# Graph aggregation with LayerNorm: row tiles in groups of twelve instead of eight, a ring of three 48 KB slots instead of eight of 16 KB, programs written out without loops

## The chip, the cores and the metric

The kernel runs on one core of a Trainium2 chip. The metric is device time in microseconds (us) for one execution; lower is better. Times of whole runs are medians over several executions; the profile comes from one execution of its own.

## The reference

`x` is 8192 x 64, `adj` is 8192 x 8192, both float32, `w` has 8192 entries and `W_agg` is 64 x 64.

```python
agg = adj @ (x @ W_agg)
y = x + w[:, None] * relu(agg) + (1 - w)[:, None] * x
out = (y - mean(y)) / sqrt(var(y) + 1e-5)      # over the 64 columns of a row
```

`adj` is 268 MB and is read once; everything else together is some 4 MB.

## The kernel before

The 8192 rows of the result are 64 row tiles of 128 rows. The contraction over 8192 columns of `adj` is cut into 64 steps `j` of 128. Before the launch the host lays `adj` out so that each transfer reads one contiguous row of bytes per partition.

**Head.** SP loads `x` in four transfers (L107) and `W_agg` twice (L109, L110), then fills the ring (L115). For eight blocks TensorE (PE) transposes two row tiles of `x` at a time (`transpose_x`, L156), ScalarE (ACT) copies the transposed block out of PSUM (L225), PE multiplies it with `W_agg` (L172), and VectorE (DVE) copies the product into `xw` (L258). Both PSUM stages have two buffers, so block b waits for the copy of block b-2. ACT loads `w` (L220) after the first transposes; DVE waits for it only after the eighth block (L261).

**Main stage.** Seven groups of eight row tiles. A group is 16 loads of 2 MB (`SUB` = 4 steps `j`, 16 KB per partition) into a ring of eight slots. `contract` (L177) multiplies: for each `j` the 128 x 64 block of `xw` is the weight, and two halves of the row tiles, 512 columns each, stream past it into the two halves of the partitions of `acc`. One float32 product shows as two MATMUL records and two LDWEIGHTS. The last one of a load frees its slot (`slot_free`), on which SP waits before it issues the load eight places on (L119). Then a group of six row tiles follows (16 loads of 1.5 MB, L126), and one of two (six loads of 2, 2, 2, 1, 0.5 and 0.5 MB, L133).

**End of a group.** ACT copies `acc` out (L231), PE turns it back with transposes (`turn_back`, L194), and DVE and ACT finish: residual, weighting, mean, variance, square root, reciprocal, scaling (L271 to L290). ACT stores the rows (L236). PE goes on with the next group as soon as its transposes are issued.

The order on each queue is that of the program. SP issues nothing but loads, ACT the load of `w` and the stores. The main groups are hardware loops (`Fori`) on SP, PE, ACT and DVE.

Of the kernel before, what the change touches and what calls it, by code (L numbers as in the profile page):

```python
# [17 lines left out]
def gnn_residual_layernorm(nc, x, adj_main, adj_mid, adj_last, w, w_agg, out):  # L18

# [20 lines left out]
    PAIRS = T // 2  # L40
    PB = 4
    BLOCKS = PAIRS // PB
    LOADS = (G + 1) * C + len(LAST_LOADS)
    assert C * SUB == T == sum(LAST_LOADS) and LAST_T0 + LAST_SLOTS == T and C % RING == 0

    DVE_PRE = 1
    DVE_GROUP = 9
    VSUM_STEP = 8

    def arrivals(load):  # L50

        return 16 * (load // RING + 1)

    ctx = ExitStack()
    with ctx:
# [36 lines left out]
        xT_done, xT_copied = sem("xT_done"), sem("xT_copied")
        xw_done, xw_copied = sem("xw_done"), sem("xw_copied")
        agg_copied = sem("agg_copied")
# [7 lines left out]
        @block.sync  # L102
        def _(sp):

            for i in range(X_PARTS):
                part = slice(i * T // X_PARTS, (i + 1) * T // X_PARTS)
                sp.dma_start(xres[:, part], x.rearrange("(p t) d -> p t d", p=P)[:, part]).then_inc(x_in[i], 16)  # L107
                if i == 0:
                    sp.dma_start(wagg2[0:D, :], w_agg).then_inc(wagg_in, 16)  # L109
                    sp.dma_start(wagg2[D:P, :], w_agg).then_inc(wagg_in, 16)  # L110
            for c in range(C):
                if c >= RING:

                    sp.wait_ge(slot_free, c - RING + 1)
                sp.dma_start(ring[:, c % RING], adj_main[0, c].rearrange("q s n -> q (s n)")).then_inc(loaded[c % RING], 16)  # L115
            with sp.Fori(1, G) as g:
                for c in range(C):

                    sp.wait_ge(slot_free, g * C + (c - RING + 1))  # L119
                    sp.dma_start(ring[:, c % RING],  # L120
                                 adj_main[bass.ds(g, 1), c].rearrange("o q s n -> (o q) (s n)")).then_inc(loaded[c % RING], 16)
            for c in range(C):
                load = MID * C + c

                sp.wait_ge(slot_free, load - RING + 1)
# [21 lines left out]
        def _(pe):  # L147
            def transpose_x(b):

                if b % (BLOCKS // X_PARTS) == 0:  # L150
                    pe.wait_ge(x_in[b * X_PARTS // BLOCKS], 16)
                if b >= 2:
                    pe.wait_ge(xT_copied, b - 1)
                for i in range(PB):
                    t = 2 * (b * PB + i)
                    last = nc.tensor.transpose(xT_ps[b % 2][:, i * P:(i + 1) * P],  # L156
                                               xres[:, t:t + 2].rearrange("p t d -> p (t d)"), ident[:])
                last.then_inc(xT_done, 1)

            pe.wait_ge(ident_ready, 1)
            transpose_x(0)
# [25 lines left out]
            def turn_back(g, n_slots):  # L188

# [3 lines left out]
                for k in range(n_slots // HALVES):  # L193
# [4 lines left out]
            with pe.Fori(0, G) as g:  # L198
                for c in range(C):
                    pe.wait_ge(loaded[c % RING], g * (16 * C // RING) + arrivals(c))  # L200
                    contract(c % RING, c * SUB, SUB, MAIN_SLOTS)
                turn_back(g, MAIN_SLOTS)
            for c in range(C):
                load = MID * C + c
                pe.wait_ge(loaded[load % RING], arrivals(load))
                contract(load % RING, c * SUB, SUB, MID_SLOTS)
            turn_back(MID, MID_SLOTS)
            j = 0
            for i, n in enumerate(LAST_LOADS):
                load = LAST * C + i  # L210
                pe.wait_ge(loaded[load % RING], arrivals(load))
                contract(load % RING, j, n, LAST_SLOTS)
                j += n
            turn_back(LAST, LAST_SLOTS)

        @block.scalar
        def _(act):

            act.wait_ge(xT_done, 1)
            act.dma_start(w_sb[:], w.rearrange("(p t) -> p t", p=P)).then_inc(w_in, 16)  # L220
            for b in range(BLOCKS):
# [3 lines left out]
                nc.scalar.copy(xT[:, b % 2], xT_ps[b % 2][:]).then_inc(xT_copied, 1)  # L225
            act.wait_ge(eps_ready, 1)

            def group(g, t0, n_slots, loads):
                width = n_slots // HALVES * P
                act.wait_ge(slot_free, loads)  # L230
                nc.scalar.copy(aggT[:, 0:width], acc[:, 0:width]).then_inc(agg_copied, 1)  # L231
                act.wait_ge(dve_step, g * DVE_GROUP + (DVE_PRE + VSUM_STEP))
                nc.scalar.activation(std[:, 0:n_slots], varsum[:, 0:n_slots], ACT.Sqrt,  # L233
                                     bias=eps[:, 0:1], scale=1.0 / D).then_inc(std_ready, 1)
                act.wait_ge(out_ready, g + 1)
                act.dma_start(out.rearrange("(p t) d -> p t d", p=P)[:, bass.ds(t0, n_slots)],  # L236
                              xres[:, bass.ds(t0, n_slots)]).then_inc(stored, 16)

            with act.Fori(0, G) as g:
                group(g, g * MAIN_SLOTS, MAIN_SLOTS, g * C + C)  # L240
            group(MID, MID_T0, MID_SLOTS, LAST * C)
            group(LAST, LAST_T0, LAST_SLOTS, LOADS)
# [3 lines left out]
        def _(dve):  # L246
            def step(instruction, count):

# [5 lines left out]

            for b in range(BLOCKS):
                dve.wait_ge(xw_done, b + 1)
                for h in range(2):
                    last = nc.vector.tensor_copy(xw[:, 2 * PB * b + h:2 * PB * (b + 1):2], xw_ps[b % 2][h][:])  # L258
# [4 lines left out]
            for i in range(X_PARTS):  # L263
                dve.wait_ge(x_in[i], 16)
            dve.wait_ge(xT_done, BLOCKS)

            def group(g, t0, n):
                base = g * DVE_GROUP + DVE_PRE
                v, s, residual = y[:, 0:n], sq[:, 0:n], xres[:, bass.ds(t0, n)]

                step(nc.vector.tensor_tensor(s, residual, over_row(one_minus_w[:, bass.ds(t0, n)]), ALU.mult), base + 1)  # L271
                step(nc.vector.tensor_tensor(residual, residual, s, ALU.add), base + 2)  # L272
                dve.wait_ge(rows_done, g + 1)

                step(nc.vector.scalar_tensor_tensor(out=v, in0=rows_ps[:, 0:n * D].rearrange("p (n d) -> p n d", d=D),  # L275
# [53 lines left out]
```

## Time and profile before

| | us |
|---|---|
| median of 3 runs | 653.82 (653.77 to 653.98) |
| span of the profiled execution, first to last instruction | 651.5 |
| busy: PE / weight loads / DVE / ACT | 496.9 / 174.3 / 58.3 / 31.4 |
| DMA: bytes moved, mean rate over the span | 272.84 MB, 419 GB/s |

The profile gives no time of its own for its execution other than the span; the median of the runs stands 2.3 us above it. In the rows below a time is in us from the start of the span unless marked ns. SPq and ACTq are the queues on which SP and ACT issue transfers; q1 holds SP's transfers, q10 ACT's, q8 the engines' instruction fetches. Text in square brackets behind an instruction is how long its engine had been idle and what ended that.

### The profile page before, as it was taken

The numbers are of one execution on the slowest core, as the hardware profiler recorded it, in microseconds if no ns is written. First come the engines' busy times: TensorE is split into PE (matmuls) and PEld (weight loads), VectorE is DVE, ScalarE is ACT, GpSimd is POOL, SyncE is SP. The second block draws the span as 40 slices with busy tenths as digits, with TensorE's granted clock in tenths as the row PEclk, the third lists the DMA queues.
The fourth block names the chain that finished last, engine by engine and source line by source line (L and its number), as shares of the span: only waits on it lengthen the run. The fifth ranks groups of instructions, "written<-read, shape, count | busy, mean of one in ns | idle before, by whom it ended". The sixth has DMA issues, their size and how long they took to land.

```text
span 651.5 us, 5854 instructions
## 1 busy us (share of the span) xinstructions
PE 496.9 (76%) x2496; PEld 174.3 (27%) x2496; DVE 58.3 (9%) x107; ACT 31.4 (5%) x41; POOL 0.7 (0%) x7
## 2 busy tenths in 40 slices
PE   6999887677777778767777777877777777777775
PEld 5733222222222122222222212212222221222245
DVE  1300012000210003000030000300003000030021
ACT  2200010000100001000020000200002000100000
POOL 0000000000000000000000000000000000000000
PEclk9999999999999999999999999999999999999999
DMA  8999999999999999999999999999999999999994
GB/s 316 433 427 428 430 424 431 432 423 433 430 426 432 425 430 433 424 431 431 425 433 423 431 433 424 428 434 426 432 424 432 432 424 432 426 425 428 422 429 164
DMA packets 21481, 272.84 MB, mean 419 GB/s; under 512 B 2656, under 2 KB 2912, under 8 KB 4576
## 3 DMA queue, kind: packets, MB, share of 16 engines
q1 hardware_dynamic: 20032, 270.57, 97.8%
q10 hardware_dynamic: 1440, 2.13, 0.9%
q8 instruction: 7, 0.11, 0.1%
q14 instruction: 2, 0.02, 0.0%
HBM read 270.60 MB, written 2.10 MB: 419 GB/s over the span
## 4 chain that ended last, share of the span: by engine, by line
DMA 80%; PE 18%; issue 0%; DVE 0%; ACT 0%; SPq 0%; ACTq 0%; DVEq 0%
DMA ring<-adj_main_dram 65%; PE acc L184 15%; DMA ring<-adj_mid_dram 9%; DMA ring<-adj_last_dram 5%; PE xw_ps L172 2%; PE xT_ps L156 1%; DMA xres<-x_dram 1%; ACT L225 0%; SPq L120 0%; ACT xT L225 0%; DVE xw L258 0%; ACTq L220 0%; PE rows_ps L194 0%; ACT std L233 0%; DVE y L279 0%
## 5 line engine op out<-in xcount | busy, mean ns | idle before, releaser
L184 PE MATMUL acc<-ring,xw 128*64 128x512 f32 (+2 forms) x2304 | 468.4, 552 | 137.3 <-DMA ring<-adj_main_dram 119.6
L184 PEld LDWEIGHTS acc<-ring,xw 128*64 128x64 f32 x2304 | 151.0, 137 | 449.2 <-issue 217.9
L275 DVE SCALAR_TENSOR_TENSOR y<-rows_ps,w_sb 128x512 f32<-128x512 f32 (+2 forms) x9 | 5.7, 632 | 560.3 <-PE rows_ps L194 560.3
L231 ACT COPY aggT<-acc 128x512 f32<-128x512 f32 (+2 forms) x9 | 4.8, 538 | 550.8 <-PE acc L184 550.8
L172 PE MATMUL xw_ps<-wagg,xT 64*128 64x64 f32 x128 | 15.5, 424 | 0.7 <-ACT xT L225 0.7
L172 PEld LDWEIGHTS xw_ps<-wagg,xT 64*128 64x128 f32 x128 | 14.2, 326 | 3.1 <-issue 2.0
L156 PE MATMUL xT_ps<-ident,xres 128*128 128x128 f32 x32 | 8.9, 433 | 5.3 <-DMA xres<-x_dram 4.8
L194 PE MATMUL rows_ps<-ident,aggT 128*128 128x128 f32 x32 | 5.4, 288 | 6.3 <-ACT aggT L231 6.3
L231 ACT ACT_TABLE_LOAD x7 | 9.0, 1283 | 11.5 <-DVE xres L290 11.4
L233 ACT ACT_TABLE_LOAD x7 | 9.0, 1283 | 0.1
L258 DVE COPY xw<-xw_ps 128x256 f32<-128x256 f32 x16 | 6.0, 419 | 24.4 <-PE xw_ps L172 24.4
L156 PEld LDWEIGHTS xT_ps<-ident,xres 128*128 128x128 f32 x32 | 5.7, 216 | 6.4 <-issue 4.8
L194 PEld LDWEIGHTS rows_ps<-ident,aggT 128*128 128x128 f32 x32 | 3.4, 140 | 13.3 <-issue 11.5
L279 DVE TENSOR_TENSOR y<-y,xres 128x512 f32<-128x512 f32 (+2 forms) x9 | 5.7, 633 | 0.3
L290 DVE TENSOR_TENSOR xres<-y,rstd 128x512 f32 (+2 forms) x9 | 5.7, 633 | 0.3
L272 DVE TENSOR_TENSOR xres<-xres,sq 128x512 f32 (+2 forms) x9 | 5.7, 632 | 0.3
L285 DVE TENSOR_TENSOR sq<-y 128x512 f32<-128x512 f32 (+2 forms) x9 | 5.7, 632 | 0.3
L282 DVE SCALAR_TENSOR_TENSOR y<-rowsum,y 128x512 f32<-128x512 f32 (+2 forms) x9 | 5.7, 632 | 0.3
L286 DVE TENSOR_REDUCE varsum<-sq 128x8 f32<-128x512 f32 (+2 forms) x9 | 5.6, 627 | 0.3
L281 DVE TENSOR_REDUCE rowsum<-y 128x8 f32<-128x512 f32 (+2 forms) x9 | 5.6, 627 | 0.3
L271 DVE TENSOR_TENSOR sq<-xres,one_minus_w 128x512 f32 (+2 forms) x9 | 5.6, 626 | 0.4 <-DVE one_minus_w L262 0.4
L225 ACT COPY xT<-xT_ps 128x512 f32<-128x512 f32 x8 | 4.6, 586 | 14.5 <-PE xT_ps L156 14.4
(11 smaller groups left out, 6.9 us busy)
## 6 DMA issues: line engine op xcount, KB each, us to landing
ring<-adj_main_dram SPq DMA_DIRECT2D x112, 2048.0 KB, 35.3
ring<-adj_mid_dram SPq DMA_DIRECT2D x16, 1536.0 KB, 27.5
ring<-adj_last_dram SPq DMA_DIRECT2D x3, 2048.0 KB, 29.0
xres<-x_dram SPq DMA_DIRECT2D x4, 512.0 KB, 6.3
out_dram<-xres ACTq DMA_DIRECT2D x7, 256.0 KB, 9.4
ring<-adj_last_dram SPq DMA_DIRECT2D x1, 1024.0 KB, 29.5
ring<-adj_last_dram SPq DMA_DIRECT2D x2, 512.0 KB, 25.8
out_dram<-xres ACTq DMA_DIRECT2D x1, 192.0 KB, 7.8
```

Source lines behind the costliest of these rows:

```text
L156: last = nc.tensor.transpose(xT_ps[b % 2][:, i * P:(i + 1) * P], xres[:, t:t + 2].rearrange("p t d -> p (t d)"), ident[:])
L172: last = nc.tensor.matmul(xw_ps[b % 2][h][:, i], xT[h * D:(h + 1) * D, b % 2, i * P:(i + 1) * P], wagg2[h * D:(h + 1) * D, :], start=True, ...
L184: last = nc.tensor.matmul(acc[h * D:(h + 1) * D, 0:width], xw[:, j], ring[:, slot, at:at + width], start=j == 0, stop=j == T - 1)
L194: last = nc.tensor.transpose(rows_ps[:, k * P:(k + 1) * P], aggT[:, k * P:(k + 1) * P], ident[:])
L231: nc.scalar.copy(aggT[:, 0:width], acc[:, 0:width]).then_inc(agg_copied, 1)
L233: nc.scalar.activation(std[:, 0:n_slots], varsum[:, 0:n_slots], ACT.Sqrt, bias=eps[:, 0:1], scale=1.0 / D).then_inc(std_ready, 1)
L258: last = nc.vector.tensor_copy(xw[:, 2 * PB * b + h:2 * PB * (b + 1):2], xw_ps[b % 2][h][:])
L272: step(nc.vector.tensor_tensor(residual, residual, s, ALU.add), base + 2)
L275: step(nc.vector.scalar_tensor_tensor(out=v, in0=rows_ps[:, 0:n * D].rearrange("p (n d) -> p n d", d=D), scalar=0.0, in1=over_row(w_sb[:, ...
L279: step(nc.vector.tensor_tensor(v, v, residual, ALU.add), base + 4)
L282: step(nc.vector.scalar_tensor_tensor(out=v, in0=over_row(rowsum[:, 0:n]), scalar=-1.0 / D, in1=v, op0=ALU.mult, op1=ALU.add), base + 6)
L285: step(nc.vector.tensor_tensor(s, v, v, ALU.mult), base + 7)
```

## The change

- Main groups of twelve row tiles (five groups of eight loads). A load is 6 MB: eight steps `j`, 48 KB per partition. The ring has three slots.
- A group of three row tiles (nine loads, 1.5 MB each but for the last two), and a last one of a single row tile, whose ten shrinking transfers all go into one ring slot and have a semaphore each. For these two groups, even and odd `j` go to the two halves of the partitions, and a product with two stacked identities adds the halves while it turns them back.
- A main load is 8 x 4 products of 384 columns, over two PSUM banks.
- `x` comes in one transfer. The two loads of `W_agg` move from SP to ACT, and the load of `w` moves to ACT's first instructions, behind them. DVE waits for `w` before the first copy of `xw`.
- `(2 - w) * x` is computed once for all rows, relu is applied by ACT in its copy for the main groups, and the square-root table of ACT is loaded once, at the start.
- The last row tile uses `bn_stats` and `bn_aggr`.
- No hardware loops.

The diff, cut to its core:

```diff
-HALVES = 2
-MAIN_SLOTS = 8
-MID_SLOTS = 6
-LAST_SLOTS = 2
-SUB = 4
-LAST_LOADS = (16, 16, 16, 8, 4, 4)
-RING = 8
-X_PARTS = 4
+HALVES = 1
+MAIN_SLOTS = 12
+MID_SLOTS = 3
+LAST_SLOTS = 1
+SUB = 8
+RING = 3
+MID_LOADS = (8, 8, 8, 8, 8, 8, 8, 5, 3)
+LAST_LOADS = (16, 13, 10, 7, 5, 4, 3, 2, 2, 2)
...
         def _(sp):
-            for i in range(X_PARTS):
-                part = slice(i * T // X_PARTS, (i + 1) * T // X_PARTS)
-                sp.dma_start(xres[:, part], x.rearrange("(p t) d -> p t d", p=P)[:, part]).then_inc(x_in[i], 16)
-                if i == 0:
-                    sp.dma_start(wagg2[0:D, :], w_agg).then_inc(wagg_in, 16)
-                    sp.dma_start(wagg2[D:P, :], w_agg).then_inc(wagg_in, 16)
...
+            sp.dma_start(xres[:], x.rearrange("(p t) d -> p t d", p=P)).then_inc(x_in, 16)
+            for load in range(G * C):
+                if load >= RING:
+                    sp.wait_ge(slot_free, load - RING + 1)
+                sp.dma_start(ring[:, load % RING],
+                             adj_main[load // C, load % C].rearrange("q s n -> q (s n)")).then_inc(loaded[load % RING], 16)
+            j = 0
+            for i, n in enumerate(MID_LOADS):
+                load = MID_LOAD0 + i
                 sp.wait_ge(slot_free, load - RING + 1)
+                sp.dma_start(ring[:, load % RING, 0:n * MID_SLOTS * P],
+                             adj_mid[j // SUB, :, j % SUB:j % SUB + n].rearrange("q s n -> q (s n)")
+                             ).then_inc(loaded[load % RING], 16)
+                j += n
+            sp.wait_ge(slot_free, LAST_LOAD0 - RING + 1)
             j = 0
+            for k, n in enumerate(LAST_LOADS):
+                sp.dma_start(ring[:, LAST_LOAD0 % RING, j * P:(j + n) * P],
+                             adj_last[:, j:j + n].rearrange("q s n -> q (s n)")).then_inc(last_loaded[k], 16)
                 j += n
...
-            def contract(slot, j0, n_j, n_slots):
-                width = n_slots // HALVES * P
-                for s in range(n_j):
+            def contract(slot, j0):
+                for s in range(SUB):
                     j = j0 + s
-                    for h in range(HALVES):
-                        at = (s * HALVES + h) * width
-                        last = nc.tensor.matmul(acc[h * D:(h + 1) * D, 0:width], xw[:, j], ring[:, slot, at:at + width],
-                                                start=j == 0, stop=j == T - 1)
+                    for b in range(BANKS):
+                        for h in range(2):
+                            at = s * COLS + (h * BANKS + b) * CHUNK
+                            last = nc.tensor.matmul(acc[h * D:(h + 1) * D, b, 0:CHUNK], xw[:, j], ring[:, slot, at:at + CHUNK],
+                                                    start=j == 0, stop=j == T - 1)
                 last.then_inc(slot_free, 1)
...
         def _(act):
-            act.wait_ge(xT_done, 1)
+            for h in range(2):
+                act.dma_start(wagg2[h * D:(h + 1) * D, :], w_agg).then_inc(wagg_in, 16)
             act.dma_start(w_sb[:], w.rearrange("(p t) -> p t", p=P)).then_inc(w_in, 16)
+            nc.scalar.preload_act_table_set("sqrt_and_others")
...
         def _(dve):
+            dve.wait_ge(ident_ready, 1)
+            nc.vector.tensor_tensor(ident2[:], ident[:, 0:D], ident[:, D:P], ALU.add).then_inc(ident2_ready, 1)
+            dve.wait_ge(w_in, 16)
+            step(nc.vector.tensor_scalar(two_minus_w[:], w_sb[:], -1.0, 2.0, ALU.mult, ALU.add), 1)
             for b in range(BLOCKS):
                 dve.wait_ge(xw_done, b + 1)
...
-            dve.wait_ge(w_in, 16)
-            step(nc.vector.tensor_scalar(one_minus_w[:], w_sb[:], -1.0, 1.0, ALU.mult, ALU.add), DVE_PRE)
...
+            step(nc.vector.tensor_tensor(xres[:], xres[:], over_row(two_minus_w[:]), ALU.mult), DVE_PRE)
...
+            v, t = y[:, 0], LAST_T0
+            dve.wait_ge(rows_done, LAST + 1)
+            step(nc.vector.tensor_scalar(v, rows_ps[:, 0:D], 0.0, w_sb[:, t:t + 1], ALU.max, ALU.mult), LAST_STEP0 + 1)
+            step(nc.vector.tensor_tensor(v, v, xres[:, t], ALU.add), LAST_STEP0 + 2)
+            step(nc.vector.bn_stats(stats[:], v), LAST_STEP0 + 3)
+            step(nc.vector.bn_aggr(mv[:], stats[:]), LAST_STEP0 + LAST_VAR_STEP)
+            dve.wait_ge(std_ready, LAST + 1)
+            step(nc.vector.reciprocal(rstd[:, 0:1], std[:, 0:1]), LAST_STEP0 + 5)
+            nc.vector.tensor_scalar(xres[:, t], v, mv[:, 0:1], rstd[:, 0:1], ALU.subtract, ALU.mult).then_inc(out_ready, 1)
```

## Rows read from the trace of the kernel before

**Rows 1.** The page: DMA share by slice; instruction queue (packets, MB, share); chain by engine.

```profile
DMA  8999999999999999999999999999999999999994
...
q8 instruction: 7, 0.11, 0.1%
...
DMA 80%; PE 18%; issue 0%; DVE 0%; ACT 0%; SPq 0%; ACTq 0%; DVEq 0%
```

**Rows 2.** The chain of waits in order of time: start, duration, what.

```profile
0.74 3.90 DMA xres<-x_dram
...
105.07 3.68 PE acc L184 x16
...
144.83 3.68 PE acc L184 x16
...
183.98 3.68 PE acc L184 x16
```

**Rows 3.** Timeline of the group of six row tiles: start, duration, instruction.

```profile
614.58 0.82 PE L184 MATMUL acc<-ring,xw 128*64 128x384 f32 x4
...
616.29 2.80 PE L184 MATMUL acc<-ring,xw 128*64 128x384 f32 x16 [0.89 <-DMA ring<-adj_mid_dram]
...
623.67 2.80 PE L184 MATMUL acc<-ring,xw 128*64 128x384 f32 x16 [0.90 <-DMA ring<-adj_mid_dram]
...
626.52 0.48 ACT L231 COPY aggT<-acc 128x384 f32<-128x384 f32 x1 [52.87 <-PE acc L184]
...
627.05 0.55 PE L194 MATMUL rows_ps<-ident,aggT 128*128 128x128 f32 x3 [0.58 <-ACT aggT L231]
```

**Rows 4.** DMA issues: size in KB, median us from issue to landing.

```profile
out_dram<-xres ACTq DMA_DIRECT2D x7, 256.0 KB, 9.4
...
out_dram<-xres ACTq DMA_DIRECT2D x1, 64.0 KB, 1.6
...
w_sb<-w_dram ACTq DMA_DIRECT2D x1, 32.0 KB, 10.8
```

**Rows 5.** Timeline of the head, PE and the ring's first issues.

```profile
3.99 6.15 SPq L115 DMA_DIRECT2D ring<-adj_main_dram  x8
...
8.24 1.97 PE L172 MATMUL xw_ps<-wagg,xT 64*128 64x64 f32 x16 [0.70 <-ACT xT L225]
...
14.14 1.97 PE L172 MATMUL xw_ps<-wagg,xT 64*128 64x64 f32 x16
...
30.66 19.69 PE L184 MATMUL acc<-ring,xw 128*64 128x512 f32 x80 [1.04 <-DVE xw L258]
```

**Rows 6.** Stretches of the head: window, length, busy (count) by engine, PEclk, DMA share, GB/s.

```profile
4.00:5.00 1.00, 0.22 (x1) 0.25 (x2) 0.00 (x0) 0.00 (x0) 0.00 (x0) 1.00 0.61 99
5.00:6.00 1.00, 0.87 (x4) 0.46 (x3) 0.00 (x0) 0.00 (x0) 0.00 (x0) 1.00 0.70 214
...
30.60:35.40 4.80, 4.74 (x12) 1.52 (x14) 1.39 (x2) 0.00 (x0) 0.00 (x0) 1.00 0.99 423
35.40:60.00 24.60, 24.60 (x116) 8.19 (x114) 0.00 (x0) 0.00 (x0) 0.00 (x0) 1.00 1.01 429
```

**Rows 7.** Timeline of the last group.

```profile
633.46 3.71 PE L184 MATMUL acc<-ring,xw 128*64 128x128 f32 x64 [1.18 <-DMA ring<-adj_last_dram]
...
638.63 7.21 PE L184 MATMUL acc<-ring,xw 128*64 128x128 f32 x128 [1.45 <-DMA ring<-adj_last_dram]
645.88 0.27 ACT L231 COPY aggT<-acc 128x128 f32<-128x128 f32 x1 [14.33 <-PE acc L184]
...
646.96 0.29 DVE L279 TENSOR_TENSOR y<-y,xres 128x128 f32<-128x128 f32 x1
...
649.50 0.36 ACTq L236 DMA_DIRECT2D out_dram<-xres  x1
```

**Rows 8.** Stretches of the end, columns as in rows 6.

```profile
640.00:641.00 1.00, 1.00 (x24) 1.00 (x22) 0.00 (x0) 0.00 (x0) 0.00 (x0) 1.00 0.85 336
...
643.00:644.00 1.00, 1.00 (x22) 1.00 (x20) 0.00 (x0) 0.00 (x0) 0.00 (x0) 1.00 0.02 8
...
650.00:652.00 2.00, 0.00 (x0) 0.00 (x0) 0.00 (x0) 0.00 (x0) 0.00 (x0) 0.50 0.11 33
```

More of the change, by code:

```diff
@@ L39, in gnn_residual_layernorm @@
     COLS = MAIN_SLOTS * P
[L40 to L48, printed above, removed]
+    HALF = MAIN_SLOTS // 2
+    BANKS = 2
+    CHUNK = HALF * P // BANKS
+    MID_BANKS = -(-MID_SLOTS * P // 512)
+    MID_CHUNK = MID_SLOTS * P // MID_BANKS
+    BLOCKS = T // 2 // PB
+    MID_LOAD0 = G * C
+    LAST_LOAD0 = MID_LOAD0 + len(MID_LOADS)
+    assert C * SUB == T == sum(MID_LOADS) == sum(LAST_LOADS) and LAST_T0 + LAST_SLOTS == T
+    DVE_PRE = 2
+    DVE_GROUP, VAR_STEP = 7, 6
+    LAST_STEP0 = DVE_PRE + LAST * DVE_GROUP
+    LAST_VAR_STEP = 4
     def arrivals(load):
@@ L186, in contract, with turn_back @@
                 last.then_inc(slot_free, 1)
-            def turn_back(g, n_slots):
+            def turn_back(g):
                 pe.wait_ge(agg_copied, g + 1)
                 pe.wait_ge(dve_step, g * DVE_GROUP + DVE_PRE)
-                for k in range(n_slots // HALVES):
+                for k in range(HALF):
                     last = nc.tensor.transpose(rows_ps[:, k * P:(k + 1) * P], aggT[:, k * P:(k + 1) * P], ident[:])
                 last.then_inc(rows_done, 1)
-            with pe.Fori(0, G) as g:
+            for g in range(G):
@@ L214, in _ @@
-            turn_back(LAST, LAST_SLOTS)
+                    load = g * C + c
+                    pe.wait_ge(loaded[load % RING], arrivals(load))
+                    contract(load % RING, c * SUB)
+                turn_back(g)
+            j = 0
+            for i, n in enumerate(MID_LOADS):
+                load = MID_LOAD0 + i
+                pe.wait_ge(loaded[load % RING], arrivals(load))
+                for s in range(n):
+                    h = (j + s) % 2
+                    for b in range(MID_BANKS):
+                        at = s * MID_SLOTS * P + b * MID_CHUNK
+                        last = nc.tensor.matmul(mid_acc[h * D:(h + 1) * D, b, 0:MID_CHUNK], xw[:, j + s],
+                                                ring[:, load % RING, at:at + MID_CHUNK], start=j + s < 2, stop=j + s >= T - 2)
+                last.then_inc(slot_free, 1)
+                j += n
@@ new lines, in _ @@
+            j = 0
+            for k, n in enumerate(LAST_LOADS):
+                pe.wait_ge(last_loaded[k], 16)
+                for s in range(n):
+                    h = (j + s) % 2
+                    last = nc.tensor.matmul(last_acc[h * D:(h + 1) * D, 0:P], xw[:, j + s],
+                                            ring[:, LAST_LOAD0 % RING, (j + s) * P:(j + s + 1) * P],
+                                            start=j + s < 2, stop=j + s >= T - 2)
+                j += n
+                if k == 0:
+                    pe.wait_ge(ident2_ready, 1)
+                    pe.wait_ge(agg_copied, MID + 1)
+                    pe.wait_ge(dve_step, MID * DVE_GROUP + DVE_PRE)
+                    for i in range(MID_SLOTS):
+                        turned = nc.tensor.matmul(rows_ps[:, i * D:(i + 1) * D], aggT[:, i * P:(i + 1) * P], ident2[:],
+                                                  start=True, stop=True)
+                    turned.then_inc(rows_done, 1)
@@ L224, in _ @@
                     act.wait_ge(xw_done, b - 1)
-                nc.scalar.copy(xT[:, b % 2], xT_ps[b % 2][:]).then_inc(xT_copied, 1)
+                nc.scalar.copy(xT[:, b % 2], xT_ps[:, b % 2]).then_inc(xT_copied, 1)
             act.wait_ge(eps_ready, 1)
[L228 to L234, printed above, removed]
-                act.wait_ge(out_ready, g + 1)
-                act.dma_start(out.rearrange("(p t) d -> p t d", p=P)[:, bass.ds(t0, n_slots)],
-                              xres[:, bass.ds(t0, n_slots)]).then_inc(stored, 16)
@@ L239, in _, with finish @@
[L239 to L242, printed above, removed]
+            out_rows = out.rearrange("(p t) d -> p t d", p=P)
+            def finish(g, t0, n_slots, var, scale, var_step):
+                act.wait_ge(dve_step, var_step)
+                nc.scalar.activation(std[:, 0:n_slots], var, ACT.Sqrt, bias=eps[:, 0:1], scale=scale).then_inc(std_ready, 1)
+                act.wait_ge(out_ready, g + 1)
+                act.dma_start(out_rows[:, t0:t0 + n_slots], xres[:, t0:t0 + n_slots]).then_inc(stored, 16)
@@ new lines, in _ @@
+            for g in range(G):
+                act.wait_ge(slot_free, g * C + C)
+                nc.scalar.activation(aggT[:].rearrange("p (b n) -> p b n", b=BANKS), acc[:, :, 0:CHUNK],
+                                     ACT.Relu).then_inc(agg_copied, 1)
+                finish(g, g * MAIN_SLOTS, MAIN_SLOTS, varsum[:], 1.0 / D, g * DVE_GROUP + (DVE_PRE + VAR_STEP))
+            act.wait_ge(slot_free, LAST_LOAD0)
+            nc.scalar.copy(aggT[:, 0:MID_SLOTS * P].rearrange("p (b n) -> p b n", b=MID_BANKS),
+                           mid_acc[:, 0:MID_BANKS, 0:MID_CHUNK]).then_inc(agg_copied, 1)
@@ L243, in _ @@
+            finish(MID, MID_T0, MID_SLOTS, varsum[:, 0:MID_SLOTS], 1.0 / D, MID * DVE_GROUP + DVE_PRE + VAR_STEP)
+            act.wait_ge(last_done, 1)
+            nc.scalar.copy(aggT[:, 0:P], last_acc[:, 0:P]).then_inc(agg_copied, 1)
+            finish(LAST, LAST_T0, 1, mv[:, 1:2], 1.0, LAST_STEP0 + LAST_VAR_STEP)
             act.wait_ge(stored, 16 * (LAST + 1))
@@ L257, in _ @@
                 for h in range(2):
[L258 removed]
+                    last = nc.vector.tensor_copy(xw[:, 2 * PB * b + h:2 * PB * (b + 1):2], xw_ps[b % 2][h])
                 last.then_inc(xw_copied, 1)
[L261 to L264 removed]
@@ L265, in _, with normalise @@
             dve.wait_ge(xT_done, BLOCKS)
-            def group(g, t0, n):
+            step(nc.vector.tensor_tensor(xres[:], xres[:], over_row(two_minus_w[:]), ALU.mult), DVE_PRE)
+            def normalise(g, t0, n, base):
+                v, s, residual = y[:, 0:n], sq[:, 0:n], xres[:, t0:t0 + n]
+                step(nc.vector.tensor_tensor(v, v, residual, ALU.add), base + 2)
+                step(nc.vector.tensor_reduce(rowsum[:, 0:n], v, AX.X, ALU.add), base + 3)
+                step(nc.vector.scalar_tensor_tensor(out=v, in0=over_row(rowsum[:, 0:n]), scalar=-1.0 / D, in1=v,
+                                                    op0=ALU.mult, op1=ALU.add), base + 4)
+                step(nc.vector.tensor_tensor(s, v, v, ALU.mult), base + 5)
+                step(nc.vector.tensor_reduce(varsum[:, 0:n], s, AX.X, ALU.add), base + VAR_STEP)
+                dve.wait_ge(std_ready, g + 1)
+                step(nc.vector.reciprocal(rstd[:, 0:n], std[:, 0:n]), base + DVE_GROUP)
+                nc.vector.tensor_tensor(residual, v, over_row(rstd[:, 0:n]), ALU.mult).then_inc(out_ready, 1)
@@ L268, in group @@
+            for g in range(G):
                 base = g * DVE_GROUP + DVE_PRE
-                v, s, residual = y[:, 0:n], sq[:, 0:n], xres[:, bass.ds(t0, n)]
-                step(nc.vector.tensor_tensor(s, residual, over_row(one_minus_w[:, bass.ds(t0, n)]), ALU.mult), base + 1)
-                step(nc.vector.tensor_tensor(residual, residual, s, ALU.add), base + 2)
                 dve.wait_ge(rows_done, g + 1)
-                step(nc.vector.scalar_tensor_tensor(out=v, in0=rows_ps[:, 0:n * D].rearrange("p (n d) -> p n d", d=D),
-                                                    scalar=0.0, in1=over_row(w_sb[:, bass.ds(t0, n)]),
-                                                    op0=ALU.max, op1=ALU.mult), base + 3)
@@ L287, in group @@
-                dve.wait_ge(std_ready, g + 1)
-                step(nc.vector.reciprocal(rstd[:, 0:n], std[:, 0:n]), base + 9)
-                nc.vector.tensor_tensor(residual, v, over_row(rstd[:, 0:n]), ALU.mult).then_inc(out_ready, 1)
-            with dve.Fori(0, G) as g:
-                group(g, g * MAIN_SLOTS, MAIN_SLOTS)
-            group(MID, MID_T0, MID_SLOTS)
-            group(LAST, LAST_T0, LAST_SLOTS)
+                for h in range(2):
+                    slots = slice(g * MAIN_SLOTS + h * HALF, g * MAIN_SLOTS + (h + 1) * HALF)
+                    last = nc.vector.tensor_tensor(
+                        y[:, h * HALF:(h + 1) * HALF],
+                        rows_ps[:, 0:MAIN_SLOTS * D].rearrange("p (k h d) -> p h k d", h=2, d=D)[:, h],
+                        over_row(w_sb[:, slots]), ALU.mult)
@@ new lines, in _ @@
+                step(last, base + 1)
+                normalise(g, g * MAIN_SLOTS, MAIN_SLOTS, base)
+            base = MID * DVE_GROUP + DVE_PRE
+            dve.wait_ge(rows_done, MID + 1)
+            step(nc.vector.scalar_tensor_tensor(out=y[:, 0:MID_SLOTS],
+                                                in0=rows_ps[:, 0:MID_SLOTS * D].rearrange("p (n d) -> p n d", d=D),
+                                                scalar=0.0, in1=over_row(w_sb[:, MID_T0:LAST_T0]),
+                                                op0=ALU.max, op1=ALU.mult), base + 1)
```

72 lines of the change are left out of this document (25 added, 47 removed).

## The prediction

> **What bounds the kernel now.** I read the page's slices first: the DMA engines are busy nine tenths or more in every slice but the first and the last, and the chain that ended last is 80% DMA [rows 1]. The time is therefore the time that the bytes take, plus what precedes the first byte, plus what follows the last, plus any hole in between. The chain in order of time gives the pace: eight loads of 2 MB take 183.98 - 144.83 = 39.15 us, 4.894 us each; with one 256 KB store among them it is 39.76 [rows 2], so a store costs what its bytes cost. PE waits for a transfer at every load: a load of 1.5 MB keeps it 2.80 us out of 3.69 [rows 3]. Its own speed matters only where it decides when a ring slot comes free and the queue has run short. So I look for what changes in the rate, at both ends, and for holes.
>
> **The rate.** 128 rows over 16 DMA engines are 8 rows per engine and load. A 16 KB row takes 4.894 / 8 = 0.6118 us [rows 2], a 12 KB row 3.69 / 8 = 0.4612, the pitch of two loads being 623.67 - 616.29 [rows 3]. The difference, 0.1506 us for 4 KB, is the price of bytes; 0.6118 - 4 x 0.1506 = 0.009 us is left per row. (At this accuracy the intercept is 0.007 to 0.011.) Rows per engine before: 8 x (112 + 16 + 6 + 4) = 1104; after: 8 x (40 + 9 + 10 + 1) = 480. Gain 624 x 0.009 = **-5.6 us**, at the same bytes. A 48 KB row is then 12 x 0.1506 + 0.009 = 1.816 us and a 6 MB load 14.53. No row above 16 KB is in this trace, so the bounds are 0 (a long row is moved in pieces) and -6.9.
>
> **x in one transfer.** The four issues of x, with the two of W_agg among them, leave the engines 39% and 30% idle in the fifth and sixth microsecond [rows 6]. With x and the first load issued back to back that goes: **-0.7 us** (0 to -0.8).
>
> **Instruction fetch.** Before, 7 fetches bring 0.11 MB [rows 1]. Without loops PE's program grows: its instructions went from 2 x 2496 executed, of which six of seven passes of a body of 512 were not fetched again (some 1900 in all), to about 6000. In proportion that is 0.25 MB more: **+0.6 us** if it falls on all engines alike, up to 5 if few of them carry it; at the end the engines finish up to 3 us apart [rows 8], so they are not loaded alike. PE uses some 130 instructions per 14.5 us, so no fetch is waited for. I find no row of a loop's back edge on the chain; removing loops gains nothing.
>
> **The tail.** The engines run out at 643 [rows 8], and PE's 128 last products run without a wait from 638.63 to 645.84 [rows 7]: the end is PE's, not the last transfer's. From 645.88 to the store's issue at 649.50 are 3.6 us, and the landing 1.6 more [rows 4] and a little to the end of the span. After: the last load is two steps, four records; by (7.21 - 3.71) / 64 = 0.055 us each and some 0.2 us for the pipeline that is 0.5 us, with 0.5 for the landing's way to PE. Then the same chain with two VectorE steps fewer (bn_stats and bn_aggr for reduce, subtract, square, reduce), 0.33 each by the pitch of [rows 7]; bn_aggr is in no row, and I take both for one step each (bounds: half, or twice). 643 + 1.0 + 3.0 + 2.0 = 649.0 instead of 651.5: **-2.5 us** (-1.8 to -3.2).
>
> **Hole at the end of the main groups.** This is the new wait that I trust most. Of one load's 64 records at 384 columns each takes (2.80 - 0.82) / 12 = 0.165 us [rows 3], so PE holds a 6 MB slot for 0.82 + 60 x 0.165 = 10.7 us. When the last main load lands, the other two slots hold loads of the next group, 2 x 3.69 = 7.4 us of transfer; the third waits, on SP's queue, for those 10.7 us. From a free slot to the first byte, and from the last byte to the waiter, together cost about 1.6 us (the last store, alone on the queue, [rows 4]; the first part of x took 3.90 for 1.2 us of bytes [rows 2], so up to 2.7). Idle: 10.7 + 1.6 - 7.4 = 4.9 us. Next PE turns the group back before it frees another slot: copy and transposes took 1.1 us for 384 columns of `acc` [rows 3], about 1.75 for 768; with 2.8 for the load, 4.55 against 3.69 of transfer: 0.9. The last ten transfers wait for one slot: landing 0.5, PE 2.8, issue 1.1, against 3.7 us still queued (loads of 5 and 3 steps): 0.7. Together **+6.5 us** (5 to 9).
>
> **Hole behind the head.** DVE now waits for w ahead of its first copy of xw; behind that wait stand all eight pairs of copies, and PE's third block waits for the first of them, because the PSUM stage has two buffers. w is the third transfer on ACT's queue. After, W_agg twice and w are 4 + 4 + 8 = 16 turns, and each turn beside a 48 KB row is 1.82 us. x fills about 2 to 7 us. Earliest: the first eight turns run beside x, w's eight beside the ring: 7 + 8 x 1.82 + 0.5 = 22. Latest: the first turn comes 2.9 us late, 12.7 turns are left when x is through: 30.6. I take the middle, 26. From block 2 on the head is PE's as before, 30.66 - 14.14 = 16.5 us [rows 5]; with 1.0 for DVE's first work PE starts the main loop at 43.5 (39.5 to 48), against 30.66. Its first 4.8 us run at half rate, as now: 12 records in 4.8 us and then 116 in 24.6 [rows 6]. The first slot is free 10.7 + 2.2 us later and its load's first byte 1.1 after that: 57.5. The queue holds x and three loads, 1.9 + 4.9 + 43.6 and some 1.6 for the engine that is last: dry at 52. Idle: **+5.5 us** (1.5 to 10). If w came before 21 us, PE would start in time (by 38 us, x itself only costs it some 2 us: landed at about 8.3, and ACT's table load is gone), and the hole would be 0.
>
> What I cost at nothing: relu in ACT's copy, the hoisted (2 - w)x (4.4 us on DVE), the longer group ends; under them lies 14.5 - 10.7 = 3.8 us of PE slack per load. Without that slack they would cost their 1 to 2 us five times.
>
> **Sum.** -5.6 - 0.7 + 0.6 - 2.5 + 6.5 + 5.5 = +3.8 on the profiled 651.5, which lies 2.3 under the median of the runs: 655.3 there, **657.6 us** as a median. With the bounds of the head's hole alone, 653.6 to 662.1.
>
> **A rule that speaks otherwise.** [Rows 4] say one row per turn. The Trainium skill, "DMA: Bandwidth & Descriptors", section on queues, rings and completion order, has a DMA engine drain a whole packet, typically 9 to 17 descriptors, from one ring before it switches. By that, w's eight rows would come in one turn, the head's hole would be 0 and the sum 652.1. The 9.4 against 1.6 us speak against it.
>
> **Rivals.** (1) *The head is covered* (ends on the other side): ACT's small rows get in ahead of the ring, w lands before 21 us. For it: ACT's queue starts at the same moment as SP's, and nothing in this trace shows a 48 KB row. Against it: [rows 4]. Without the hole: -1.7, 652.1, just faster. 25%. (2) *Long rows are moved in pieces* of at most 16 KB: no gain in rate, but turns stay at 0.61 us and w lands at 13; -0.7 + 0.6 - 2.5 + 6.5 = +3.9, 657.7, from another cause. 10%. (3) *PE's clock and the fetches*: the granted clock fell to half, 0.50, after PE's end at 646.5 [rows 8]; after the change PE idles 3.8 us per load instead of 1.2. If the clock falls ahead of the last main load, its slot comes 2.2 us later, and fetches that pile up on few engines add 2 to 4: 662 to 664. 10%. The forecast has the remaining 55%.
>
> **Numbers.** 0.2% is 1.3 us, about what a measurement of this kernel can tell from no change: faster below 652.5, slower above 655.1. Rival 1 is faster in two thirds of its cases and the same in the rest; the forecast's low end gives 5% to faster, 10% to no change. Faster 0.22, same 0.18, slower 0.60. The range reaches down to rival 1 with a shorter hole at the group end and up to the late w: 650.8 to 662.5; the likeliest case's own is 653.6 to 662.1.
>
> **What would show it.** Right: q1 rows of 48 KB at 27 GB/s per engine; w landing 20 to 30 us after its issue; DVE's first copy of xw waiting for it; first main product near 43; DMA share dropping for some 5 us at 52, and again some 7 us after the last main load lands; PE idle 3.8 us per main load; DMA's end about 6 us before the end of the span. Wrong: main products from 33 on (rival 1); a main load at 14.7 us (rival 2); main records at twice their length ahead of the last group (rival 3). A hole at the group end under 3 us, or none, would make the sum wrong by as much.

## The result and the profile after

| | us |
|---|---|
| before, median of 4 runs | 653.9 (653.77 to 654.04) |
| after, median of 4 runs | 673.1 (671.91 to 675.26) |
| ratio after to before | 1.030, 95% interval 1.028 to 1.032 |
| span of the profiled execution after | 670.1 |

The change makes the kernel 19 us slower; 657.6 was forecast. The direction and the places were right, the sizes were not. The page of the kernel after: the DMA share by slice and the rate, which answer to [rows 1], with PE's granted clock, and the instruction fetches.

```profile
PEclk9999989889788989889998979898979898989998
DMA  9992999999999999999999999999999999997795
GB/s 377 448 429 86 432 423 432 449 429 426 438 423 428 441 437 426 428 439 421 440 444 428 421 428 438 429 434 441 429 428 429 432 429 446 426 425 291 250 365 232
...
q8 instruction: 23, 0.38, 0.2%
```

Two places stand out: the fourth slice (86 GB/s) and the four last. Between them the rate is 421 to 449 GB/s, about as before. The granted clock is below nine tenths in 18 of the 40 slices, which it never was before. The chain of waits in order of time (start, duration, what), which answers to [rows 2], says what stood at these places:

```profile
1.95 30.35 DMA w_sb<-w_dram
...
49.79 44.04 PE bank L179 x256
...
568.39 10.56 PE bank L179 x64
...
612.00 10.56 PE bank L179 x64
622.59 0.82 ACT aggT L258
623.41 0.04 issue
623.45 0.87 PE bank L188 x6
...
635.74 4.22 PE bank L206 x16
```

The head is now a wait of 30 us for `w`, 32 KB, and the main products begin at 49.8 where they began at 30.7 [rows 5]. At the end the last main load holds its slot until 622.6. The stretches at both places (window, length, busy and count of PE, PEld, DVE, ACT and POOL, granted clock, DMA share, GB/s):

```profile
48.00:52.00 4.00, 3.14 (x18) 1.74 (x18) 3.05 (x4) 0.00 (x0) 0.00 (x0) 1.00 0.57 246
52.00:56.00 4.00, 4.00 (x18) 1.44 (x17) 2.07 (x1) 0.00 (x0) 0.00 (x0) 1.00 0.00 0
56.00:60.00 4.00, 4.00 (x28) 1.73 (x26) 0.00 (x0) 0.00 (x0) 0.00 (x0) 1.00 0.02 4
60.00:64.00 4.00, 4.00 (x28) 1.71 (x26) 0.00 (x0) 0.00 (x0) 0.00 (x0) 1.00 0.38 111
64.00:68.00 4.00, 4.00 (x28) 1.79 (x26) 0.00 (x0) 0.00 (x0) 0.00 (x0) 1.00 0.72 283
...
612.00:616.00 4.00, 4.00 (x26) 1.85 (x28) 0.00 (x0) 0.00 (x0) 0.00 (x0) 1.00 0.84 353
616.00:620.00 4.00, 4.00 (x28) 1.79 (x26) 0.00 (x0) 0.00 (x0) 0.00 (x0) 1.00 0.12 52
620.00:624.00 4.00, 3.09 (x21) 1.41 (x18) 0.00 (x0) 0.81 (x1) 0.00 (x0) 1.00 0.12 28
624.00:628.00 4.00, 4.00 (x28) 1.86 (x27) 3.53 (x5) 0.00 (x0) 0.00 (x0) 1.00 0.92 351
628.00:632.00 4.00, 4.00 (x28) 1.57 (x23) 3.46 (x5) 0.30 (x1) 0.00 (x0) 1.00 0.86 261
```

The DMA engines are idle while PE is fully busy. That is what a ring looks like that has run dry because PE holds the slots. Summed over the first five windows (4 x (0.43 + 1.00 + 0.98 + 0.62 + 0.28)) a mean engine loses 13.2 us at the head, over the last five 8.6.

### The profile page after: what moved, and what is told of

Read it like the earlier page. It is cut to its first block, busy times and chain, and to the rows that moved or that the text cites. A ratio compares the mean times of both kernels' runs of the same rounds, so it can differ in the third digit from the quotient of the medians.

```text
span 670.1 us, 6264 instructions
## 1 busy us (share of the span) xinstructions
PE 523.6 (78%) x3014; PEld 233.9 (35%) x3014; DVE 49.7 (7%) x78; ACT 12.9 (2%) x23; POOL 0.7 (0%) x7
## 3 DMA queue, kind: packets, MB, share of 16 engines
q10 hardware_dynamic: 1312, 2.16, 0.8%
## 4 chain that ended last, share of the span: by engine, by line
DMA 66%; PE 33%; DVE 0%; issue 0%; ACT 0%; ACTq 0%; DVEq 0%
DMA ring<-adj_main_dram 58%; PE bank L179 27%; DMA w_sb<-w_dram 5%; DMA ring<-adj_mid_dram 2%; PE bank L168 2%; PE bank L206 1%; PE bank L215 1%; DMA ring<-adj_last_dram 1%; PE bank L152 1%; DVE xw L286 0%; ACTq L237 0%; PE bank L188 0%; ACT aggT L258 0%; PE bank L225 0%; PE bank L232 0%
## 5 line engine op out<-in xcount | busy, mean ns | idle before, releaser
L179 PE MATMUL bank<-ring,xw 128*64 128x384 f32 x2560 | 462.4, 524 | 104.0 <-DMA ring<-adj_main_dram 103.2
L179 PEld LDWEIGHTS bank<-ring,xw 128*64 128x64 f32 x2560 | 192.0, 147 | 372.2 <-issue 245.9
L206 PE MATMUL bank<-ring,xw 128*64 128x384 f32 x128 | 23.1, 514 | 6.0 <-DMA ring<-adj_mid_dram 6.0
L168 PE MATMUL bank<-wagg,xT 64*128 64x64 f32 x128 | 15.5, 423 | 8.8 <-DVE xw L286 8.8
L152 PE MATMUL bank<-ident,xres 128*128 128x128 f32 x32 | 8.9, 433 | 16.6 <-DMA xres<-x_dram 8.6
L168 PEld LDWEIGHTS bank<-wagg,xT 64*128 64x128 f32 x128 | 14.2, 325 | 11.1 <-issue 11.1
L206 PEld LDWEIGHTS bank<-ring,xw 128*64 128x64 f32 x128 | 9.3, 144 | 19.3 <-issue 10.2
L152 PEld LDWEIGHTS bank<-ident,xres 128*128 128x128 f32 x32 | 5.7, 217 | 17.7 <-issue 8.6
L215 PE MATMUL bank<-ring,xw 128*64 128x128 f32 x128 | 9.1, 311 | 2.2 <-DMA ring<-adj_last_dram 2.2
L215 PEld LDWEIGHTS bank<-ring,xw 128*64 128x64 f32 x128 | 8.5, 158 | 2.9 <-DMA ring<-adj_last_dram 2.9
L286 DVE COPY xw<-bank 128x256 f32<-128x256 f32 x16 | 6.0, 419 | 11.3 <-PE bank L168 11.2
L302 DVE TENSOR_TENSOR xres<-y,rstd 128x768 f32<-128x768 f32 (+1 forms) x6 | 5.2, 858 | 0.2
L294 DVE TENSOR_TENSOR y<-y,xres 128x768 f32<-128x768 f32 (+1 forms) x6 | 5.2, 858 | 0.2
```

What stands on the lines that cost most here:

```text
L152: last = nc.tensor.transpose(xT_ps[:, b % 2, i * P:(i + 1) * P], xres[:, t:t + 2].rearrange("p t d -> p (t d)"), ident[:])
L168: last = nc.tensor.matmul(xw_ps[b % 2][h][:, i], xT[h * D:(h + 1) * D, b % 2, i * P:(i + 1) * P], wagg2[h * D:(h + 1) * D, :], start=True, ...
L179: last = nc.tensor.matmul(acc[h * D:(h + 1) * D, b, 0:CHUNK], xw[:, j], ring[:, slot, at:at + CHUNK], start=j == 0, stop=j == T - 1)
L206: last = nc.tensor.matmul(mid_acc[h * D:(h + 1) * D, b, 0:MID_CHUNK], xw[:, j + s], ring[:, load % RING, at:at + MID_CHUNK], start=j + s < ...
L215: last = nc.tensor.matmul(last_acc[h * D:(h + 1) * D, 0:P], xw[:, j + s], ring[:, LAST_LOAD0 % RING, (j + s) * P:(j + s + 1) * P], start=j ...
L294: step(nc.vector.tensor_tensor(v, v, residual, ALU.add), base + 2)
```

## The experiments

Three theories stood against each other. **A**: these two holes are the loss. **B**: the loss is PE's clock, which was granted at 0.93 on average instead of 1.00. **C**: the longer programs, written out without loops, bring fetches that delay the transfers. The first two runs each undo one part of the change, the third alters the ring, and the fourth takes one part of the change into the kernel before.

**e1: only the wait moves.** VectorE waits for `w` behind the copies of `xw` again.

```diff
         def _(dve):
...
-            dve.wait_ge(w_in, 16)
-            step(nc.vector.tensor_scalar(two_minus_w[:], w_sb[:], -1.0, 2.0, ALU.mult, ALU.add), 1)
             for b in range(BLOCKS):
...
+            dve.wait_ge(w_in, 16)
+            step(nc.vector.tensor_scalar(two_minus_w[:], w_sb[:], -1.0, 2.0, ALU.mult, ALU.add), 1)
             dve.wait_ge(xT_done, BLOCKS)
```

> Only VectorE's wait for w (with the small product that needs it) goes back behind the eight copies of xw. Theory A (holes in the transfers: the ring runs dry at 53 us because the head waits for w): W_agg still lands at 17 us on ACT's queue, so PE's first product stays at 18.7, but the main products start 22.4 later, at 41, instead of 49.8; the first slot is free at 54.7 and the hole shrinks from 11.5 to about 3 us: 673.1 - 8.6 = 664.5 us. Theory B (the loss is PE at half clock, the granted mean being 0.93): the clock in the main stage is as before, and the time stays within 1 us of 673.

Measured: 664.1 us (661.95 to 664.41), 9.0 less than after. The timeline has the first main products at 41.1, as A had it:

```profile
41.10 39.38 PE L179 MATMUL bank<-ring,xw 128*64 128x384 f32 x226 [0.86 <-DVE xw L284]
```

The mean clock is still 0.93, so the clock did not bring these 9 us back: B falls for this part.

**e2: only the queue moves.** `W_agg` and `w` are issued by SP, behind `x` and ahead of the ring; the wait stays where the change put it.

```diff
             sp.dma_start(xres[:], x.rearrange("(p t) d -> p t d", p=P)).then_inc(x_in, 16)
+            for h in range(2):
+                sp.dma_start(wagg2[h * D:(h + 1) * D, :], w_agg).then_inc(wagg_in, 16)
+            sp.dma_start(w_sb[:], w.rearrange("(p t) -> p t", p=P)).then_inc(w_in, 16)
...
         def _(act):
-            for h in range(2):
-                act.dma_start(wagg2[h * D:(h + 1) * D, :], w_agg).then_inc(wagg_in, 16)
-            act.dma_start(w_sb[:], w.rearrange("(p t) -> p t", p=P)).then_inc(w_in, 16)
```

> Only the queue of W_agg and w changes: SP issues them behind x and ahead of the ring. Theory A: both land by 10 us, main products start at 33 to 34, the first slot is free at 47, ahead of the ring's end at 53: no hole in the head, 673.1 - 11.5 = 661.6 us (660.5 to 662.5). The hole at the end of the main groups stays. Theory B: within 1 us of 673.

Measured: 659.0 us (658.78 to 662.09), 14.1 less than after, where A gave 11.5 less. `w` lands 6.7 us after its issue and the main products begin at 32.75. The fourth slice is as full as its neighbours; what is left is the end.

```profile
DMA  9999999999999999999999999999999999996796
```
```profile
w_sb<-w_dram SPq DMA_DIRECT2D x1, 32.0 KB, 6.7
```
```profile
32.75 33.90 PE L182 MATMUL bank<-ring,xw 128*64 128x384 f32 x192 [0.86 <-DVE xw L286]
```

**e3: six slots of 24 KB** instead of three of 48 KB, with everything else of the change, the late `w` included. The group of three has ten loads instead of nine, and `adj_mid` is laid out by partition for them.

```diff
-SUB = 8
-RING = 3
-MID_LOADS = (8, 8, 8, 8, 8, 8, 8, 5, 3)
+SUB = 4
+RING = 6
+MID_LOADS = (8, 8, 8, 8, 8, 8, 6, 4, 4, 2)
...
-            sp.wait_ge(slot_free, LAST_LOAD0 - RING + 1)
+            sp.wait_ge(slot_free, LAST_LOAD0 - RING + 2)
...
+        last_slots = ring[:, LAST_LOAD0 % RING:LAST_LOAD0 % RING + 2].rearrange("p r n -> p (r n)")
```

> The ring is six slots of 24 KB (four steps j per load) instead of three of 48 KB; the group of three has ten loads, the last tile takes two slots. Queues and waits of the head stay. Theory A: a turn on ACT's queue takes 0.92 us, w lands near 20 us, main products start near 38, the first slot is free by 46: no hole in the head; at the end of the main groups five slots of queue stand against 5.4 us of PE: no hole there. 328 more rows per engine cost 2.9 us: 673.1 - 11.5 - 8 + 2.9 = 656.5 us. If only the clock mattered (B), the holes would stay where they are and the gain would come from PE's records alone. If the fetches mattered most (C), at most a few us would come back: above 668.

Measured: 648.9 us (648.79 to 648.87), ratio to before 0.992 (0.991 to 0.994): faster than both kernels, and 7.6 below what A gave. Its slices have no gap; `w`'s issue, and three main loads by the start of their products:

```profile
DMA  9999999999999999999999999999999999999996
```
```profile
w_sb<-w_dram ACTq DMA_DIRECT2D x1, 32.0 KB, 18.9
```
```profile
305.43 5.38 PE L181 MATMUL bank<-ring,xw 128*64 128x384 f32 x32 [0.24 <-DMA ring<-adj_main_dram]
312.73 5.38 PE L181 MATMUL bank<-ring,xw 128*64 128x384 f32 x32 [1.92 <-DMA ring<-adj_main_dram]
320.04 5.38 PE L181 MATMUL bank<-ring,xw 128*64 128x384 f32 x32 [1.93 <-DMA ring<-adj_main_dram]
```

A load of 3 MB takes 7.30 us, so the smaller rows cost what the fit of the prediction said (8 x (6 x 0.1506 + 0.009) = 7.30). The expectation had taken 11.5 us for the hole behind the head and 8 for the one at the end. With e2's 14.1 and e5's 11.2 in their place it would have been 650.7; the 1.8 us that are left were not looked into.

**e4: the kernel before, its loops written out.** The four `Fori` become Python loops.

```diff
-            with pe.Fori(0, G) as g:
+            for g in range(G):
...
```

> The kernel before with its four hardware loops written out, nothing else. Theory C (fetches of the longer programs, 16 KB each, delay single DMA engines): fetches go from 7 to some 20 and the last engine ends 3 to 4 us later: 657 to 658 us. Rival: they ride along or hit engines evenly: 653.9 us within 0.8.

Measured: 656.8 us, ratio 1.0044 (1.003 to 1.006), 2.9 us slower, with 19 fetches. In the kernel before, C holds; for the kernel after it stands as a smaller third part, by analogy. Which engine's program it is, **e9** (all loops but PE's written out) and **e10** (PE's alone) tell:

> The kernel before with the loops of SP, ACT and DVE written out and PE's loop kept. Theory C (the fetches of PE's longer program cost e4's 2.9 us): 7 to 9 fetches, 653.9 us within 0.6. Rival (another engine's unrolled program, or the loss of some pacing that the loops gave): 656 to 657.

> The kernel before with PE's loop alone written out. Theory C: some 18 fetches, the last DMA engine ends 3 us later, 656.5 to 657 us as in e4. Rival: 653.9 us within 0.6.

Measured: e9 653.9 us, ratio 0.9998 (0.999 to 1.001); e10 657.0, ratio 1.0047 (1.003 to 1.006). It is PE's program alone. The fetches of e9 and of e10, and e10's last stretches:

```profile
q8 instruction: 7, 0.11, 0.1%
```
```profile
q8 instruction: 19, 0.31, 0.2%
```
```profile
640.00:641.00 1.00, 0.92 (x18) 0.67 (x14) 0.00 (x0) 0.00 (x0) 0.00 (x0) 1.00 0.83 338
...
644.00:645.00 1.00, 1.00 (x22) 1.00 (x20) 0.00 (x0) 0.00 (x0) 0.00 (x0) 1.00 0.44 172
645.00:646.00 1.00, 1.00 (x22) 1.00 (x20) 0.00 (x0) 0.00 (x0) 0.00 (x0) 1.00 0.08 33
646.00:647.00 1.00, 1.00 (x24) 1.00 (x22) 0.00 (x0) 0.00 (x0) 0.00 (x0) 1.00 0.06 25
```

Before, the last engine was through shortly after 643 [rows 8]. Now the mean share is still 0.44 up to 645, and 0.06, which is one engine of 16, past 646. The bytes (0.2 MB, half a microsecond) do not explain it, an uneven load would, since a load counts as landed when its last engine is done. That the fetches fall on few engines is inferred from this spread; the views do not name engines, and no run changed the fetches without changing PE's program.

**e5: larger loads for the group of three**, on e2: four loads in place of nine (`adj_mid` is laid out by partition for it).

```diff
-MID_LOADS = (8, 8, 8, 8, 8, 8, 8, 5, 3)
+MID_LOADS = (20, 20, 12, 12)
...
-                             adj_mid[j // SUB, :, j % SUB:j % SUB + n].rearrange("q s n -> q (s n)")
+                             adj_mid[:, j:j + n].rearrange("q s n -> q (s n)")
```

> On e2 (weights on SP), the group of three row tiles comes in four loads of 20, 20, 12 and 12 steps (30, 30, 18 and 18 KB rows) instead of nine of 8 steps and less. Theory A (the hole at the end of the main groups: two queued loads of 1.5 MB last 7.4 us, PE holds the slot for 10.6): the two queued loads now last 18.4 us, so PE frees the slot in time and no hole of over 1 us is left in that stretch: 8 to 10 us off e2's 659.0, 649 to 651 us. Rival (the last stretch is slow because PE is slow in it, at half clock): larger loads make PE start later, and the time stays at 659 or rises.

Measured: 647.7 us (646.80 to 648.38), 11.2 less than e2 (the kernel before moved by 0.1 us between the two measurements); ratio to before 0.990 (0.988 to 0.992), the fastest kernel here. The stretches around the end of the main groups, in e2 and then in e5 (both end the last main load's products between 610 and 612):

```profile
600.00:604.00 4.00, 4.00 (x22) 1.66 (x20) 0.00 (x0) 0.00 (x0) 0.00 (x0) 0.82 0.46 194
604.00:608.00 4.00, 4.00 (x28) 1.83 (x26) 0.00 (x0) 0.00 (x0) 0.00 (x0) 1.00 0.04 18
608.00:612.00 4.00, 3.09 (x22) 1.38 (x18) 0.00 (x0) 0.81 (x1) 0.00 (x0) 1.00 0.28 43
```
```profile
600.00:604.00 4.00, 4.00 (x16) 1.57 (x14) 0.00 (x0) 0.00 (x0) 0.00 (x0) 0.55 0.96 415
604.00:608.00 4.00, 4.00 (x28) 1.71 (x26) 0.00 (x0) 0.00 (x0) 0.00 (x0) 1.00 1.05 453
608.00:612.00 4.00, 3.36 (x22) 1.23 (x18) 0.00 (x0) 0.59 (x1) 0.00 (x0) 1.00 0.79 338
```

PE is no faster in e5, its clock is even lower (0.55 in the first window), and the transfers go on. The hole was the short queue.

**e6: PE kept busy**, on e2, by products that nothing reads:

```diff
+            def keep_busy():
+                for i in range(10):
+                    h = i % 2
+                    nc.tensor.matmul(bank[h * D:(h + 1) * D, 1, 0:384], xw[:, i], xw[:, 0:6].rearrange("p t d -> p (t d)"),
+                                     start=True, stop=True)
```

> On e2, PE computes ten products of 384 columns into an unused PSUM bank after each main load but the last (values not used): 3.3 us of the some 4 us in which it idles. Theory B (the clock): the granted mean goes from 0.92 to nearly 1 and the time falls by over 5 us, below 654. Theory A: the half-clock stretches lie beside transfers and cost nothing in the main stage; the holes at the end stay, and the time is 659 within 1.5 us. If the filler were too long, PE would pass 14.5 us per load and the time would rise.

Measured: 661.1 us (659.12 to 661.96), 2.1 more than e2, at a mean granted clock of 0.992:

```profile
PEclk9999999999999999999999999999999998999988
```
```profile
q8 instruction: 29, 0.48, 0.3%
```

With the clock up in the main stage nothing is won; B falls for it. The executions of e2 and e6 overlap, so the 2.1 us more are not clear of their scatter. In the two profiled ones, 3.1 us apart, half of the difference stands at the last row tile, for which the filler no longer runs: its first products took 1.6 us longer in e6 (645.62) than in e2 (644.02).

```profile
645.62 3.54 PE L228 MATMUL bank<-ring,xw 128*64 128x128 f32 x32 [3.62 <-DMA ring<-adj_last_dram]
```
```profile
644.02 1.97 PE L218 MATMUL bank<-ring,xw 128*64 128x128 f32 x32 [2.11 <-DMA ring<-adj_last_dram]
```

The granted clock was 0.50 in the first 2 us of that stretch in e6, and 1.00 in e2. What the six more fetches and the filler itself cost was not separated; a gain from the clock of a microsecond or two could hide under them, one of 5 could not.

**e8: e3 with e2's queue.**

> e3 (six slots of 24 KB) with W_agg and w on SP behind x. Theory A: in e3 the first slot was free before the ring ran dry although w landed only at 21 us, so an earlier w buys nothing: 648.9 within 0.7 us. If the late w still cost something that the profile does not show as a hole, 646 or less.

Measured: 649.0 us, ratio 0.992 (0.991 to 0.994), the same as e3. With slots of 24 KB the late `w` costs nothing. It lands at 20.9 in e3 and the main products begin at 38.3, but PE then holds the first slot for half as many products, and the DMA share stays at 0.96 or more in every 4 us from 36 to 64.

## Why the prediction was wrong

The forecast was 15.5 us short. Three terms were too small: the hole behind the head by 8.6 us, the hole at the end of the main groups by 4.7, and the fetches by an estimated 3.5.

**Rate: right.** Main loads start their products 14.54 us apart (568.39 to 612.00 are three), 14.53 was worked out, and e3's 24 KB rows fit the same line. 40 x (14.54 - 3 x 4.894) = -5.7 us. Rival 2, long rows moved in pieces, is out: it had `w` land at 13.

**Hole behind the head: the mechanism right, the size wrong; the main step that failed.** "I take the middle, 26": `w` landed at 32.3, later than the latest bound. Issues on ACT's queue in the kernel after:

```profile
wagg<-w_agg_dram ACTq DMA_DIRECT2D x2, 16.0 KB, 12.1
w_sb<-w_dram ACTq DMA_DIRECT2D x1, 32.0 KB, 30.4
...
DMA to landing us min/median/max: 7.9/12.1/16.3
```

The last line is that of the two `W_agg`: they took 7.9 and 16.3 us to land, issued at 0.73 and about 1.3. So the first landed at 8.6, with `x`, and its four rows and nothing more fitted beside `x`. Twelve turns were left, each beside a 48 KB row: 8.6 + 12 x 1.82 = 30.4, 2 us less than measured. Most of these 2 us lie before the second `W_agg`, which landed at 17.6: 9.0 us after the first, where four turns are 7.3. The eight turns of `w` then took 14.7, where 14.5 were worked out. The price per turn was right: with 24 KB rows `w` lands 11.5 us sooner (30.4 against 18.9), and 12.6 turns of 0.91 us are that.

The step that failed is the assumption that up to eight of ACT's small rows would get their turns beside `x`; the middle, 26, counted on some of them. In the kernel after, only four did, and the first of them to land came no sooner than `x` itself. Even the latest bound was too early. The row of `w` itself in [rows 4] pointed that way: 10.8 - 1.6 - 8 x 0.61 leaves 4.3 us before its first row, where the working took 2.9 from the stores.

By the rule of the Trainium skill, "DMA: Bandwidth & Descriptors", section on queues, rings and completion order, that an engine drains a whole packet of typically 9 to 17 descriptors before it switches, the eight rows of `w` would have come in one turn. By an estimate of three turns of 1.82 us, one for each of ACT's transfers, `w` would then have landed near 14, some 18 us earlier. The 14.7 us beside 48 KB rows, and 7.5 for the same eight rows beside e3's 24 KB rows (13.4 to 20.9), speak against that for rows on ACT's queue. The profile counts one packet per row there: 1312 for 1152 rows, and 16 more for each of ten transfers. If those are the packets that the rule means, a turn per packet fits the runs and only the typical size does not.

```profile
q10 hardware_dynamic: 1312, 2.16, 0.8%
```

From there the working held: 32.3 + 17.5 gives 49.8, and PE began at 49.79. The hole cost 14.1 us by e2, against 5.5 (1.5 to 10). With PE's start at 49.8 the prediction's own sum makes it 11.8; the other 2.3 us are open.

**Hole at the end of the main groups: mechanism right, price 11.2 us (e5) instead of 6.5 (5 to 9).** PE held the last main slot for 10.56 us as worked out. The term counted three clean gaps. The whole stretch is slow in the profile: after the gap the share is up again, but not the rate.

```profile
636.00:640.00 4.00, 3.93 (x16) 1.26 (x14) 0.00 (x0) 0.00 (x0) 0.00 (x0) 0.68 0.99 409
640.00:648.00 8.00, 5.60 (x32) 2.12 (x33) 0.00 (x0) 0.00 (x0) 0.00 (x0) 1.00 0.99 398
```

In these 12 us, with one or two short loads queued, the engines moved some 400 GB/s instead of 430. And PE, idle for 3.5 us before 635.74, begins that load at a granted clock of 0.50, the lower of its two levels, takes 4.22 us instead of 2.80 [rows 3], and frees its slot that much later. Here the clock of rival 3 reaches the path. The profiles show it at two more places, which the share of the whole hides: e2's last main load and, in the kernel after, the first products of the last row tile (1.97 us in e2):

```profile
598.13 12.18 PE L182 MATMUL bank<-ring,xw 128*64 128x384 f32 x64 [4.00 <-DMA ring<-adj_main_dram]
```
```profile
655.57 3.63 PE L215 MATMUL bank<-ring,xw 128*64 128x128 f32 x32 [2.19 <-DMA ring<-adj_last_dram]
```

The first load held its slot for 12.18 us (granted 0.50 in its first 1.9 us and 0.63 in the next 2), against 10.56 in the kernel after, so some 1.6 of the 11.2 us that e5 took off e2 are not in the kernel after. The second ran at a granted clock of 0.52 to 0.54. I did not split the 4.7 us further.

**Fetches: 0.6 taken, about 4 by an estimate from e10.** e10 has 3.1 us for 12 more fetches, the kernel after has 16 more; no run took them out of the kernel after. "If it falls on all engines alike" was the wrong end of the bound (up to 5), although [rows 8] already showed the engines unevenly loaded. That removing the loops gains nothing was right (e9); what the prediction mis-sized is what the fetches cost that they had saved.

**Tail: right.** The transfers end shortly before 664 and the span at 670.1, some 6.3 us, against 8.5 before: -2.2, and -2.5 was forecast. No term held the 1.7 us that the first products of the last row tile took longer than in e2.

Sum of the terms: -5.7 + 4 - 2.2 + 14.1 + 11.2 = +21.4; the kernel lost 19.2. The gain from x, which no run measured alone, is left out. The price in e5 includes five loads fewer and e2's 1.6 us, and so is no pure hole; the fetches are an estimate. That the sum comes this close is partly luck.

## What to carry to other kernels

Size a ring by time, not by bytes: the bytes queued behind the slot that the consumer holds must last longer than it holds it, also where large loads give way to small ones. Six slots of half the size cost an estimated 2.9 us in row overhead here, and the kernel came out 24 us faster.

A small transfer that something waits for belongs on the queue of the bulk, ahead of it: there `w` landed in 6.7 us. On the other queue each of its rows took about the time of one bulk row here, and large rows made that dear.

## What was not expected of the hardware

- A small row takes about as long as the bulk row beside it. Behind 32 KB of `W_agg`, the 32 KB of `w` took 18.9 us to land beside rows of 24 KB and 30.4 beside rows of 48 KB; with nothing ahead on its queue, 10.8 beside rows of 16 KB.
- Writing out PE's loop, which brings twelve more instruction fetches of 16 KB, cost a kernel bound by its transfers 3.1 us, six times what the 0.2 MB take.
- In the main stage a low granted clock of PE cost nothing measurable: e6, at a mean of 0.992, took 661.1 us and e2, at 0.924, 659.0. At the end, where PE frees the last slots and does the last products, it lay on the path.
